# Stacking two graphs along the partitions in the last two layers of a four-layer graph network

## What is computed

```python
# L2: batch norm over all graphs and nodes, then a linear layer and a normalised Laplacian
mean = Hf.mean(axis=0); var = jnp.mean((Hf - mean) ** 2, axis=0)
Hn = (Hf - mean) * jax.lax.rsqrt(var + BN_EPS) * gamma + beta
d = A.sum(axis=2)
A_norm = jnp.sqrt(d)[:, :, None] * A * jax.lax.rsqrt(d)[:, None, :]
out = leaky_relu((eye - A_norm) @ (Hn @ W + b), 0.01)
# L3: two dense layers, messages along the edges, and a gated update
m = relu(h @ W1 + b1); m = relu(m @ W2 + b2)
msg = relu(A @ m)
gi = msg @ W_ih.T + b_ih;  gh = h @ W_hh.T + b_hh
r = sigmoid(i_r + h_r); z = sigmoid(i_z + h_z); n = tanh(i_n + r * h_n)
out = (1 - z) * n + z * h
```

## Time and profile before

| | us |
|---|---|
| median of three runs (3181.69 to 3190.41) | 3188.65 |
| the profiled execution | 3183.33 |
| its span, first to last instruction | 3181.5 |
| VectorE busy | 2805.6 (88%) |
| TensorE busy | 2234.6 (70%) |
| ScalarE busy | 1987.2 (62%) |
| final stages, from the last x_all of the second layer to the end | 308.9 |

### The profile page before, as it was taken

One profiled execution on the slowest core, in us unless ns is written; L12 is line 12 of the kernel. 1 busy time (PEld: TensorE's weight loads), 2 busy tenths in 40 slices (PEclk: granted clock), 3 DMA queues, 4 the chain that ended last, 5 costly groups with the idle time before them and its releaser, 6 DMA issues.

```text
span 3181.5 us, 45583 instructions
## 1 busy us (share of the span) xinstructions
PE 2234.6 (70%) x16081; PEld 1004.7 (32%) x16234; DVE 2805.6 (88%) x5398; ACT 1987.2 (62%) x3077; POOL 12.4 (0%) x24
## 2 busy tenths in 40 slices
PE   0000014387888888898888888888898889776996
PEld 0000002232333333333333333333333333225664
DVE  7999998999989999999999999999999999546776
ACT  2111443178887878787788787778788777741322
POOL 0000000000000000000000000000000000000000
PEclk6555557688989989898999989899999989886777
DMA  3001000000101001010100101010100100000101
GB/s 68 0 0 26 31 0 0 22 15 20 38 7 35 12 29 26 17 33 12 36 11 31 21 21 34 11 38 8 34 13 29 34 10 19 10 20 27 40 26 40
DMA packets 126916, 72.05 MB, mean 23 GB/s; under 512 B 95513, under 2 KB 110059, under 8 KB 126699
## 3 DMA queue, kind: packets, MB, share of 16 engines
q1 hardware_dynamic: 122570, 68.23, 8.4%
q10 hardware_dynamic: 4128, 1.05, 0.2%
HBM read 41.05 MB, written 15.58 MB: 18 GB/s over the span
## 4 chain that ended last, share of the span: by engine, by line
DVE 57%; PE 27%; ACT 8%; issue 6%; SPq 1%; DMA 1%; DVEq 0%; ACTq 0%
PE ring L624 5%; DVE picked L1527 5%; PE rows L665 4%; ACT hot L1078 3%; PE found_bank L677 3%; PE bcast L637 3%; DVE picked L1519 3%; DVE picked L1511 3%; DVE picked L1521 3%; DVE picked L1493 3%; DVE keys L1329 3%; DVE keys L1330 3%; PE bank L919 2%; DVE picked L1499 2%; DVE delta L1370 2%
## 5 line engine op out<-in xcount | busy, mean ns | idle before, releaser
L1078 ACT ACTIVATE hot<-bcast,consts 128x1024 f16<-128x1024 f32 x744 | 831.5, 1118 | 112.8 <-PE bcast L637 112.8
L624 PE MATMUL ring<-member,neigh_t 128*128 128x512 bf16 x1925 | 495.4, 396 | 40.8 <-issue 16.0
L665 PE MATMUL rows<-hot,table 128*64 128x512 f16 x3072 | 515.8, 416 | 0.0
L1071 ACT ACTIVATE prod<-rows 128x512 f32<-128x512 f32 x720 | 432.1, 600 | 10.1 <-PE rows L665 10.1
L637 PE MATMUL bcast<-idx_t,consts 32*128 32x512 f16 x1488 | 309.5, 413 | 169.4 <-ACT hot L1078 167.6
L654 PE MATMUL rows<-fine_rows,consts 32*128 32x512 bf16 x768 | 314.2, 409 | 18.1 <-DMA fine_rows<-turned 18.0
L624 PEld LDWEIGHTS ring<-member,neigh_t 128*128 128x128 bf16 x2048 | 189.3, 102 | 325.0 <-issue 110.0
L562 PE MATMUL ring<-identb,adj_b 128*128 128x128 bf16 x256 | 33.2, 294 | 358.7 <-ACT adj_b L974 347.3
L677 PE MATMUL found_bank<-prod,consts 128*32 128x512 f32 x1536 | 233.1, 683 | 11.2 <-ACT prod L1071 10.4
L637 PEld LDWEIGHTS bcast<-idx_t,consts 32*128 32x128 f16 x1488 | 70.6, 92 | 510.7 <-ACT hot L1078 338.0
L1527 DVE TENSOR_TENSOR picked<-picked 128x3072 uint16<-128x3072 uint16 (+2 forms) x192 | 209.5, 1091 | 11.2
(11 more groups left out here) (347 smaller groups left out, 4324.7 us busy)
## 6 DMA issues: line engine op xcount, KB each, us to landing
late<-in_adj_dram SPq DMA_DIRECT2D x16, 1024.0 KB, 5.4
adjt_d<-neigh_t SPq DMA_DIRECT2D x16, 512.0 KB, 2.7
fine_rows<-turned SPq DMA_DIRECT2D x512, 8.0 KB
fine_rows<-turned SPq DMA_DIRECT2D x512, 16.0 KB
turned<-adjt_d SPq DMA_DIRECT2D x16, 512.0 KB, 3.6
adj_s<-adjt_d SPq DMA_DIRECT2D x16, 512.0 KB, 4.0
xt_d<-keys SPq DMA_DIRECT2D x2, 1024.0 KB, 10.4
parts_d<-parts SPq DMA_DIRECT2D x4, 512.0 KB, 6.9
```

The lines of the kernel that those rows point to most:

```text
L624: ins = mm(ring[u % 2][:, :], kept_t[:, j, P * i:P * i + P], member[:, j, n // 2, 512 * (n % 2):512 * (n % 2) + 512], start=(j == 0), stop ...
L665: ins = mm(rows[u % 2][C * h:C * h + C, :], table[:, s, GROUPS * h + g8, :], hot[:, u % HOT, h, :], start=False, stop=(s == 1), skip_group ...
L1071: run(prod[:, u % DEEP, :], rows[u % 2][:, :], ACT.Relu).then_inc(S["prod_by_act"], 1)
L1078: run(hot[:, u % HOT].rearrange(flat), spread_bank(l, u)[0][:, 0:2, :].rearrange(flat), ACT.Relu, bias=eq_bias[:, :]).then_inc(S["hot_read ...
```

## The change

Both graphs of a half-group now lie side by side as one pair `a`: 128 features (two graphs of 64) wherever one graph had 64.

- A transpose takes 128 columns and gives 128 partitions, graph 0 on partitions 0 to 63 and graph 1 on 64 to 127: four for a pair, not eight.
- The dense and linear layers use block-diagonal 128 x 128 weights (`w3a_two`, `w3b_two`, `w2f_s`), one product for both graphs. Their biases no longer ride as a 65th row: w3b's is a product of a row of ones with `b3b_two` (L931), w2's is added by VectorE from `b2f_s`, the gates' is a product of ones with `b_gates` (L973).
- The messages write two column groups of one bank (partitions 0 to 63 and 64 to 127), alternating. The gates use two row groups (`tile_position`) and their own four banks, `gates`.
- Evictions and VectorE operations span 512 columns rather than twice 256. ScalarE evicts the second dense layer, so VectorE's L1859 goes. `cur` is no longer copied from `x_all`.
- Both halves' batch statistics are joined by a product with `mean_of`; six weights are loaded twice, to both halves of the partitions.
- The turns are written out: no hardware loop, constants as wait targets.

Core of the diff, TensorE, ScalarE, VectorE and SP in turn:

```diff
-                             (gamma_s[:, :], gamma.rearrange("(c o) -> c o", o=1)), (beta_s[:, :], beta.rearrange("(c o) -> c o", o=1)),
-                             (w2_s[:, :], w2), (b2_s[C:C + 1, :], b2.rearrange("(o c) -> o c", o=1)), (w3a_s[:, :], w3a),
-                             (b3a_s[:, :], b3a.rearrange("(c o) -> c o", o=1)), (w3b_s[0:C, :], w3b),
-                             (w3b_s[C:C + 1, :], b3b.rearrange("(o c) -> o c", o=1)),
+                             (b2_s[:, :], b2.rearrange("(o c) -> o c", o=1)), (b3b_s[:, :], b3b.rearrange("(o c) -> o c", o=1)),
...
+            for g in range(2):
+                at = slice(C * g, C * g + C)
+                for dst, src in ((gamma_s, gamma.rearrange("(c o) -> c o", o=1)), (beta_s, beta.rearrange("(c o) -> c o", o=1)),
+                                 (b3a_s, b3a.rearrange("(c o) -> c o", o=1)), (w2_s, w2), (w3a_s, w3a), (w3b_s, w3b)):
+                    sp.dma_start(dst[at, :], src).then_inc(S["w_loaded"], 16)
...
+                if old is not None:
+                    a, w = old, old % 2
+                    pe.wait_ge(S["x3_ready"], a + 1)
                     for i in range(NT):
+                        ins = tp(bank[1][:, 0, P * i:P * i + P], cur[w][:, i, :], ident[:, :])
+                    ins.then_inc(S["ht_ps"], 1)
+                    pe.wait_ge(S["ht_ev"], a + 1)
+                    mm(bank[1][:, 1, :], w3a_two[:, :], cur_t[w][:, :], start=True, stop=True).then_inc(S["m1_ps"], 1)
+                    pe.wait_ge(S["m1_ev"], a + 1)
+                    for i in range(NT):
+                        mm(bank[1][:, 0, P * i:P * i + P], mid_t[w][:, P * i:P * i + P], w3b_two[:, :], start=True, stop=False)
+                        ins = mm(bank[1][:, 0, P * i:P * i + P], ones_row[:, :], b3b_two[:, :], start=False, stop=True)
                     ins.then_inc(S["m2_ps"], 1)
...
+                    pe.wait_ge(S["cut2_ready"], a + 1)
                     for j in range(NT):
                         for s in range(3):
-                            ins = mm(bank[q][0:C, 0, :], cut[q][:, s, j, :], adj_s[q][:, j, :], start=(j == 0 and s == 0), stop=(j == NT - 1 and s == 2))
+                            for g in range(2):
+                                ins = mm(bank[1][C * g:C * g + C, 1, :], cut[w][:, s, j, C * g:C * g + C], adj_s[2 * w + g][:, j, :],
+                                         start=(j == 0 and s == 0), stop=(j == NT - 1 and s == 2), skip_group_check=True)
                     ins.then_inc(S["msg_ps"], 1)
...
-                    for i in range(NT):
-                        dst = bank[q][:, i // 2, 256 * (i % 2):256 * (i % 2) + 256]
-                        mm(dst[:, 0:3 * C], msg_t[q][:, P * i:P * i + P], wih_s[:, :], start=True, stop=False, skip_group_check=True)
-                        mm(dst[:, 0:2 * C], cur_t[q][:, P * i:P * i + P], whh_s[:, 0:2 * C], start=False, stop=True, skip_group_check=True)
-                        ins = mm(dst[:, 3 * C:4 * C], cur_t[q][:, P * i:P * i + P], whh_s[:, 2 * C:3 * C], start=True, stop=True, skip_group_check=True)
+                        dst = [gates[:, 2 * g + i // 2, 256 * (i % 2):256 * (i % 2) + 256] for g in range(2)]
+                        for g in range(2):
+                            mm(dst[g], ones_row[:, :], b_gates[:, :], start=True, stop=False, skip_group_check=True)
+                        for g in range(2):
+                            r = slice(C * g, C * g + C)
+                            mm(dst[g][:, 0:3 * C], msg_t[w][r, of], wih_s[r, :], start=False, stop=False, skip_group_check=True, tile_position=(C * g, 0))
...
+            stage(0, None)
+            for a in range(1, PAIRS):
+                stage(a, a - 1)
+            stage(None, PAIRS - 1)
...
-            for q in range(SLOTS):
-                for t in (cur_t, mid_t, msg_t):
-                    did(v.memset(t[q][C:C + 1, :], 1.0))
+            did(v.tensor_copy(stage_two[0:96], stage_w[0:96, 0:4, :].unsqueeze(2).to_broadcast([96, 4, 2, C])))
+            for g in range(2):
+                did(tt(mean_of[:, C * g:C * g + C], ident[:, 0:C], ident[:, C:2 * C], ALU.add))
+            need(count[0])
+            then(ts(mean_of[:, :], mean_of[:, :], 0.5, None, ALU.mult))
             tell("l1_done")
...
+                    dve.wait_ge(S["lin_ps"], a + 1)
+                    then(tt(lin[w][:, :, :], of_bank(bank[0][:, 1, :]), b2f_s[:, :].unsqueeze(1).to_broadcast([P, NT, 2 * C]), ALU.add))
+                    then(tt(wide(scl[w][:, :, :]), wide(lin[w][:, :, :]), per_graph(inv_root, a), ALU.mult))
+                    cut3(w, "cut_ready")
...
+                    dve.wait_ge(S["rz_ready"], 2 * a + 2)
+                    dve.wait_ge(S["cut2_ready"], a + 1)
```

More of the change, by code:

```diff
@@ L317, in build, with two @@
[L317 to L323, removed]
+        def two(name, shape, dt):
+            return [sb(f"{name}{i}", shape, dt) for i in range(2)]
+        cur = two("cur", [P, NT, 2 * C], F32)
+        cur_t = two("cur_t", [P, N], F32)
@@ new lines, in build @@
+        mid_t = two("mid_t", [P, N], F32)
+        msg_t = two("msg_t", [P, N], F32)
+        lin = two("lin", [P, NT, 2 * C], F32)
+        scl = two("scl", [P, NT, 2 * C], F32)
+        rest = two("rest", [P, NT, 2 * C], F32)
+        cut = two("cut", [P, 3, NT, 2 * C], BF16)
+        gate = two("gate", [P, NT, 2, 2 * C], F32)
+        cand = two("cand", [P, NT, 2 * C], F32)
+        stat = two("stat", [P, NT, 2, 6], F32)
+        mom = two("mom", [P, NT, 2, 2], F32)
+        dev = two("dev", [P, 2, NT, 2], F32)
@@ L882, in _ @@
+            for a in range(PAIRS):
+                if a >= 2:
+                    pe.wait_ge(S["bn_read"], a - 1)
                 for i in range(NT):
-                    ins = tp(bank[b % 2][0:C, 0, P * i:P * i + P], x_all[:, i, b, :], ident[:, :])
+                    ins = tp(bank[a % 2][:, 0, P * i:P * i + P], both(x_all, a, i), ident[:, :])
                 ins.then_inc(S["bT_ps"], 1)
+            pe.wait_ge(S["bn_half"], 1)
+            mm(gates[:, 0, 0:2], mean_of[:, :], bn_two[:, :], start=True, stop=True).then_inc(S["bn_ps"], 1)
@@ L939, in _ @@
-            stage(half(0, 0), [])
-            stage(half(0, 1), half(0, 0))
-            with pe.Fori(1, B // SLOTS) as g0:
-                stage(half(g0, 0), half(g0 - 1, 1))
-                stage(half(g0, 1), half(g0, 0))
-            stage([], half(B // SLOTS - 1, 1))
+                if new is not None:
+                    a, w = new, new % 2
+                    for g in range(2):
+                        pe.wait_ge(adjs_in[2 * w + g], 16 * (a // 2 + 1))
+                    pe.wait_ge(S["cut_ready"], a + 1)
+                    for g in range(2):
+                        for i in range(NT):
+                            to = P * i + C * g
+                            for j in range(NT):
+                                for s in range(3):
+                                    ins = mm(bank[0][:, 0, to:to + C], adj_s[2 * w + g][:, j, P * i:P * i + P], cut[w][:, s, j, C * g:C * g + C],
+                                             start=(j == 0 and s == 0), stop=(j == NT - 1 and s == 2))
+                    ins.then_inc(S["agg_ps"], 1)
@@ new lines, in stage @@
+                if old is not None:
+                    a, w = old, old % 2
+                    act.wait_ge(S["gate_ps"], a + 1)
+                    for g in range(2):
+                        run(gate[w][:, :, g, :], gates[:, 2 * g:2 * g + 2, :].rearrange("p k (i n) -> p (k i) n", i=2)[:, :, 0:2 * C], ACT.Sigmoid).then_inc(S["rz_ready"], 1)
+                    act.wait_ge(S["cand_ready"], a + 1)
+                    run(cand[w][:, :, :].rearrange(flat), scl[w][:, :, :].rearrange(flat), ACT.Tanh).then_inc(S["new_ready"], 1)
@@ L1908, in _ @@
+            stage(0, None, None)
+            stage(1, 0, None)
+            for a in range(2, PAIRS):
+                stage(a, a - 1, a - 2)
+            stage(None, PAIRS - 1, PAIRS - 2)
+            stage(None, None, PAIRS - 1)
             restart()
```

348 lines of the change are left out of this document (179 added, 169 removed).

## The result

The changed kernel takes **3204.7 us** (median of 15 runs, 3192.7 to 3212.3) against 3185.8 us for the kernel before in the same session (15 runs, 3181.7 to 3190.4): a ratio of **1.0058, 95% interval 1.0047 to 1.0069**, so about 18.5 us slower. The forecast was 9.6 us slower, with a range from 3178 to 3220. The direction and the range held; the size was half of what came.

What follows compares the result with a forecast made beforehand. A turn's chain of waits, TensorE steps then VectorE and ScalarE latency, was taken as the bound. Start +3.5, preparation -8.3, first turn +3.1, seven turns +5.5, last turn +5.8 sum to +9.6: 3198.2 us, range 3178 to 3220.

Steps and rivals of the forecast that it cites:

- start: Six weight loads issued twice on SP delay the store that VectorE's sort waits for: +3.5 us, bounds 0 and 3.6.
- preparation: Before the first turn: fewer memsets and statistics, against added joining of the halves' moments: -8.3 us, between -6 and -9.
- first turn: No other pair hides its waits: 19.7 us where 16.6 stood, +3.1.
- w3a, a turn: First dense product of a turn: one product instead of two, but its ReLU eviction is waited for; no change.
- w3b, a turn: Four 128-column products, each followed by a one-row bias product, 0.72 us each: 5.75, +2.15 us; bounds +1.3 and +2.15.
- w2 and messages, a turn: Four w2 products, -1.65 us; messages in two overlapping column groups take 4.5 us, -2.9, bounds 4.0 and 7.4.
- aggregation, a turn: The pair's 96 products must all end: 3.1 us instead of 1.52, +1.6; up to 5.3 at the low clock.
- to the next w3a, a turn: After aggregation, the formerly hidden gates hold up the sigmoid: 12.8 us, +1.6; bounds 11.0 and 15.
- last turn: One graph's sigmoid no longer starts during the other's gates: 35.0 us against 29.2, +5.8, bounds +3 and +9.
- The two overlap rivals: Gates' row groups don't overlap: +29 us, chance 0.13; messages' column groups don't overlap: +33 us, chance 0.05.
- the term for the gates: Gate products after the aggregation, priced at the full clock: 2.1 us a tile, 8.4 in all, with the sigmoid waiting.
- The rival of the low clock: Low clock reaches into aggregation and gates: 3.1 becomes 5.3, 8.4 doubles; +10 us a turn, +90 in sum, chance 0.04.

Runs made afterwards that it cites:

- the two experiments on order: Changed kernel with all of graph 0's products ahead of graph 1's: in the messages 3218.2 us (1.0092), within each tile of the gates 3282.3 us (1.0295).

## Why the prediction was half right

Each step against what the profiled execution shows, in us against before:

| step | forecast | measured |
|---|---|---|
| start | +3.5 | +3.7 at the sort, +4.5 at the preparation |
| preparation | -8.3 | -9.3 |
| first turn | +3.1 | +2.4 |
| w3a, a turn | 0 | +0.7 in the turn shown, +0.3 in the mean |
| w3b, a turn | +2.15 | +2.25 |
| w2 and messages, a turn | -4.55 | -4.8 |
| aggregation, a turn | +1.6 | +1.45 |
| to the next w3a, a turn | +1.6 | +2.6 in the turn shown, +3.4 in the mean |
| seven turns | +5.5 | +18.8 |
| last turn | +5.8 | +10.5 |
| output | 0 | -0.4 |
| sum | +9.6 | +26.5 (profiled), +18.5 (medians) |

**Right.** The start, the preparation, w3b's 0.72 a product, the column groups of the messages overlapping (24 products in 3.4 to 4.8 us in the seven turns, 5.4 to 6.5 when one graph follows the other), the row groups of the gates overlapping, and that the gates would come onto the chain and release the sigmoid. A tile of the gates takes 1.98 us at the full clock, 2.1 forecast; inside it two errors offset each other, as the two bias products take 1.06 (0.95 forecast) and the six others with the changes between groups 0.92 (1.14). The two overlap rivals are excluded by these numbers and by the two experiments on order. The reason given against the first of them, that weights load beside a running product only for another row group, is no support here: in the kernel before, the first aggregation has weight loads busy for 5.15 of its 5.28 us beside products that all use 128 rows. Of the preparation's sum, -0.2 is a term that nothing in the prediction explains.

**Wrong: the clock in the term for the gates, and with it the last turn.** Turns of 31 to 33 us and gates of 8 were to show that the prediction was right; they came out at 34.2 and 10.7. The prediction priced aggregation and gates at the full clock, since the earlier trace rows shows them there, and gave 0.04 to the low clock reaching into them, with the reason that the gates hold the clock up now. They did, but they were other products: 65 rows each, with the bias among them. The change turns that row into one-row products that take half of the gates' time, and with them the clock fell: in the turn shown, the last tile took 3.69 instead of 1.98. The prediction counted these products, gave them their columns' price, and didn't ask what they do to the clock. In the mean the gates took 10.7 us in the seven turns instead of the forecast 8.4; w3a, "no change" in the forecast, takes 2.85 us to w3b in every turn, where before it took 1.9 to 3.6, 2.6 in the mean, because its ReLU stands open and its product has no full-clock half left. In the last turn the clock was full for 3.5 us only (0.54) and the gates took 12 us rather than 8.4.

The rival of the low clock, at +90 us and a chance of 0.04, came true in part: it was to be low throughout aggregation and gates, and it was low in a part of the gates alone.

**Partly luck: the number.** The kernel with 128 rows in the gates' bias products is the case that the prediction had priced, with the gates at the full clock. It came out at +0.6 us (1.0002), not at +9.6. So the lost clock cost 18 us, and the rest of the forecast was some 9 us too dear. The trace of that kernel shows where: a turn is 30.8 us in the mean, not 32.3. The clock stays up into w3a, which takes 0.5 less than before where no change was forecast, the aggregation takes 2.8 where 3.1 stood, and from there to the next w3a it is 11.9 where 12.8 stood. The two errors have opposite signs, and each cancelled part of the other. Where in the gates the clock falls, if it does, differs from turn to turn (gates of 7.8 to 12.3 us), and by the spread of the times probably from run to run; with 128 rows the spread shrinks to 4 us.

**Right in size, wrong in reason:** w3b. I read 0.61 for the alternation at the low clock from the earlier trace rows and added columns, "as the columns must pass". The sum came out, but the columns are not the reason: the same columns take 0.43 with 128 rows on both sides. The rows were there to see it: a w2 product at the low clock takes less (3.50 for eight) than the 0.61 of the dense layer's alternation with as few columns. 2.3 of the 5.86 us of w3b are for changing the number of rows.

**Still open:** whether the clock answers to the number of rows itself or to something else that one-row operands change; only three numbers of rows were tried, at one place, and one turn of the changed kernel kept the clock with one-row products. Nor was it tried what w3b's full rows alone would do to the changed kernel.

## What to carry to other kernels

A bias as a one-row fp32 product is cheap only where TensorE has time to spare. Once such products come onto the chain they cost the change of rows on either side (0.29 us each next to 128-row products at the low clock here) and may cost the clock for what follows; spread the bias over 128 rows, or better, open the sum with a small bf16 product while TensorE waits for something else. And when a change moves work from beside the chain onto it, price it at the clock that this work will have in its new surroundings, not at the one it had in the old: ask what of it keeps the clock up.

## What the hardware showed that I had not expected

- The granted clock fell from 2.4 to 1.2 GHz in the middle of uninterrupted TensorE work, 6 to 10 us after it had risen, in six of seven turns, where half of the time in the gates went to one-row products; with the same products over 128 rows it stayed up for about 17 us in all seven and outlasted 3.4 us of idleness. With 32 rows it fell in the gates in one turn of seven.
- Changing between one-row and 128-row fp32 products of 128 columns costs 0.29 us each time at the low clock (0.72 against 0.43).
- Products of fp32 in two row groups overlap in full: six products of two graphs in alternation take 0.92 us, the three of one graph alone 0.91.
- Messages of one graph after the other are 1.7 us a turn longer, and gates with unchanged products came out 1.4 us shorter in the same execution, because the clock stayed up in more of them.
- A start mark on one region of a bank undoes what another region of the bank has opened.
